# Return totals of two tiles made in one GpSimd addition, in a macaron block of two feed-forward layers around a quaternion memory

## The reference, cut to what matters

```python
keys = (x @ Wk.T + bk).reshape(B, L, 64, 4)
keys = keys / max(norm(keys, axis=-1), 1e-12)
values = (x @ Wv.T + bv).reshape(B, L, 64, 4)
bound = quat_mul(values, keys)
memory = jnp.cumsum(bound, axis=1)
retrieved = quat_mul(memory, quat_conj(keys)).reshape(B, L, D)
retrieved = retrieved / jnp.sqrt(positions)[None, :, None]
normed = layernorm(retrieved) * ln_g + ln_b
return x + (normed @ Wo.T + bo)
```

## Time and profile before

| What | Value |
|---|---|
| Time, median of 3 runs | 648.37 us (646.26 to 649.11) |
| Profiled execution: time | 648.11 us |
| Profiled execution: span of its instructions | 646.4 us |
| Mean granted TensorE clock | 0.994 |
| VectorE busy, whole span | 565.1 us (87%), 1168 instructions |
| GpSimd busy, whole span | 539.8 us (84%), 626 instructions |
| PE busy, whole span | 612.6 us (95%) |

### The profile page before, as it was taken

The page is one execution under the profiler, slowest core; times in us unless marked ns, Lnnn a source line. Parts: engine busy times, 40 slices in busy tenths (PEclk is TensorE's granted clock), DMA queues, the critical chain, the costliest instruction groups (busy, mean ns, idle before and its releaser), DMA issues.

```text
span 646.4 us, 12285 instructions
## 1 busy us (share of the span) xinstructions
PE 612.6 (95%) x3341; PEld 521.1 (81%) x3341; DVE 565.1 (87%) x1168; ACT 468.2 (72%) x858; POOL 539.8 (84%) x626
## 2 busy tenths in 40 slices
PE   6989999999987999999999999998877999999997
PEld 5878989989865787777878787777666899898996
DVE  6979999998869999999999999999848788787773
ACT  5666776767567888888888888887365777677662
POOL 4588898897848999999999999998826988889863
PEclk9989999999999999999999999999899999999999
DMA  8740000000000000000000000000000110110111
GB/s 251 238 132 1 0 0 0 0 0 1 1 1 1 1 2 0 0 0 0 0 0 0 0 0 0 0 1 0 2 0 2 67 65 32 65 65 32 65 66 66
DMA packets 19273, 18.66 MB, mean 29 GB/s; under 512 B 1328, under 2 KB 19248, under 8 KB 19248
## 3 DMA queue, kind: packets, MB, share of 16 engines
q1 hardware_dynamic: 19248, 18.36, 8.8%
HBM read 9.97 MB, written 8.39 MB: 28 GB/s over the span
## 4 chain that ended last, share of the span: by engine, by line
PE 45%; POOL 25%; issue 18%; DVE 7%; ACT 3%; POOLq 1%; DMA 0%; DVEq 0%; ACTq 0%
PE bank L1228 25%; PE bank L1259 16%; POOL rhalf L286 7%; POOL ret L293 6%; POOL kact L275 5%; POOL bhalf L268 4%; PE bank L1242 4%; POOL bhalf L266 1%; ACT xn L778 1%; POOL rhalf L284 1%; DVE xk L410 1%; POOL xr_lo L1084 1%; DVE xn L613 1%; DVE kact L418 0%; POOL rstd L1077 0%
## 5 line engine op out<-in xcount | busy, mean ns | idle before, releaser
L1259 PE MATMUL bank<-wffn,kact 128*128 128x256 f32 x512 | 118.0, 384 | 6.5 <-DVE kact L418 4.1
L1318 PE MATMUL bank<-wkv,m_xnT 128*128 128x256 f32 x480 | 116.4, 385 | 2.4 <-ACT m_xnT L882 2.4
L1259 PEld LDWEIGHTS bank<-wffn,kact 128*128 128x128 f32 x512 | 96.0, 192 | 19.5 <-DVE kact L418 4.5
L1318 PEld LDWEIGHTS bank<-wkv,m_xnT 128*128 128x128 f32 x480 | 88.8, 190 | 24.2 <-ACT m_xnT L882 8.8
L299 POOL TENSOR_TENSOR xk_lo<-xk,xk_hi 128x1024 fp32r<-128x1024 f32 x30 | 71.1, 2370 | 43.7 <-ACT xk_hi L786 43.4
L1091 POOL TENSOR_TENSOR res<-res,gating_buffers 128x1024 f32 (+1 forms) x31 | 74.6, 2408 | 13.5 <-DVE gating_buffers L425 13.0
L1084 POOL TENSOR_TENSOR xr_lo<-xr,xr_hi 128x1024 fp32r<-128x1024 f32 x32 | 76.0, 2374 | 7.6 <-ACT xr_hi L792 6.2
L613 DVE TENSOR_TENSOR xn<-bank,khat 128x1024 f32<-128x1024 f32 x64 | 77.7, 1216 | 2.2
L778 ACT ACTIVATE xn<-res,shift,rstd 128x256 f32 (+1 forms) x128 | 66.5, 592 | 15.3 <-POOL shift L1079 11.0
L613 DVE TENSOR_TENSOR gating_buffers<-bank,khat 128x1024 f32<-128x1024 f32 x64 | 77.4, 1211 | 0.0
L1228 PE MATMUL bank<-wffn_hi,xr_hi 128*128 128x256 f32 x256 | 72.1, 282 | 0.0
(11 more groups left out here) (135 smaller groups left out, 1603.8 us busy)
## 6 DMA issues: line engine op xcount, KB each, us to landing
res<-x SPq DMA_DIRECT2D x15, 512.0 KB, 4.2
out<-res SPq DMA_DIRECT2D x15, 512.0 KB, 2.9
res<-x SPq DMA_DIRECT2D x2, 256.0 KB, 2.9
out<-res SPq DMA_DIRECT2D x2, 256.0 KB, 2.2
wffn<-w_k SPq DMA_DIRECT2D x1, 256.0 KB, 4.6
wffn<-w_r SPq DMA_DIRECT2D x1, 256.0 KB, 5.3
wo<-w_o SPq DMA_DIRECT2D x1, 256.0 KB, 5.6
wffn<-w_v SPq DMA_DIRECT2D x1, 256.0 KB, 5.8
```

The source lines that it names most:

```text
L1259: last = nc.tensor.matmul(dst[:, i, :], x[:, f, i * P:(i + 1) * P], wffn[:, w, f, :], start=f == 0, stop=f == FC - 1)
L1318: last = nc.tensor.matmul(dst[:, i, :], m_xnT[:, f, i * P:(i + 1) * P], wkv[:, f, col:col + D], start=False, stop=f == FC - 1, skip_group_ ...
```

## The change

The totals of the return of both tiles of a step are made in one addition of 2 x 256 = 512 elements. It stands where the total of tile 1 stood, in the next step behind the first half of the bind sum of tile 0; the total of tile 0 at the end of its own step is left out. One semaphore counts the merged totals instead of one for each tile. VectorE's ln_stats waits for it once, ahead of the statistics of tile 0. ret_half waits for it before it writes rhalf again. retrieve waits for the second return half instead of the total, before it writes the products again.

```diff
-        rprod_done, rhalf_done, ret_done = for_tiles("rprod"), for_tiles("rhalf"), for_tiles("ret")
+        rprod_done, rhalf_done, ret_done = for_tiles("rprod"), for_tiles("rhalf"), sem("m_ret_done")
...
                 engine.wait_ge(rprod_done[i], s + 1)
-                need(engine, ret_done[i], s)
+                need(engine, ret_done, s)
...
-        def ret_total(engine, j, b, i):
+        def ret_total(engine, j, b):
+
             s = 2 * j + b
-            engine.wait_ge(rhalf_done[i], s + 1)
+            for i in range(2):
+                engine.wait_ge(rhalf_done[i], s + 1)
             need(engine, m["normed_done"], s - 1)
-            engine.tensor_tensor(ret[:, b, i, :], rhalf[:, i, 0, :], rhalf[:, i, 1, :], ALU.add).then_inc(ret_done[i], 1)
+            engine.tensor_tensor(ret[:, b, :, :], rhalf[:, :, 0, :], rhalf[:, :, 1, :], ALU.add).then_inc(ret_done, 1)
...
                     need(dve, m["normed_done"], s - 1)
+                    dve.wait_ge(ret_done, s + 1)
                     for i in range(2):
-                        dve.wait_ge(ret_done[i], s + 1)
                         nc.vector.bn_stats(n_st[:, b, i, :], ret[:, b, i, :]).then_inc(m["st_done"], 1)
...
                     s = 2 * j + b
-                    need(dve, ret_done[i], s)
+                    need(dve, rhalf_done[i], s)
                     dve.wait_ge(upto_done[i], s + 1)
...
                         if behind:
-                            ret_total(nc.gpsimd, *at(j, b, -1), 1)
+                            ret_total(nc.gpsimd, *at(j, b, -1))
                         if ahead:
                             bind_half(nc.gpsimd, *at(j, b, 1), 0, 1)
...
                         if ahead:
                             bind_half(nc.gpsimd, *at(j, b, 1), 1, 0)
-                        ret_total(nc.gpsimd, j, b, 0)
                         if ahead:
                             bind_half(nc.gpsimd, *at(j, b, 1), 1, 1)
...
-            ret_total(nc.gpsimd, NP - 1, 1, 1)
+            ret_total(nc.gpsimd, NP - 1, 1)
```

## The result

The changed kernel takes 673.66 us, the median of four runs (672.57 to 677.05), against 648.74 us for the kernel before in its four (646.26 to 649.18). The ratio is 1.040, with a 95% interval of 1.035 to 1.045. The forecast was 674.4 us, in a range of 669.5 to 680.5.

A forecast was written before the change was run, and what follows sets the result against it. VectorE was taken to set the step, in a loop with GpSimd's total; 29 x 0.88 + 0.47 = 26.0 us on top of 648.37 us gave 674.4 us, range 669.5 to 680.5.

The forecast's parts named there:

- The loop: VectorE's bind product, GpSimd's bind half and total, VectorE's statistics to next bind product form a loop giving the 8.54 us step.
- The price of 512 elements: GpSimd's merged total: 1.28 us, from a line between additions of 256 and 1024 elements.
- The bounds of 1.19 and 1.46: Limits in us for GpSimd's merged total: half a 1024 addition, and two additions of 256.
- The sum per step: VectorE's statistics 0.88 us late per step: 0.56 from the longer addition, 0.32 from the first statistic's lost cover.
- The sum: Whole memory stage: 29 steps at 0.88 us plus 0.47 for step 3, 26.0 us slower.
- The saving at step 3: At step 3 GpSimd's bind half was 0.41 us late; one addition fewer removes that, so it pays 0.47 us.
- GpSimd's relief is worth nothing: GpSimd's saving of 0.14 us per step falls into its gap before bhalf L266, only lengthening its idle time.
- the rival in which GpSimd bounds: Memory stage: 31 merged totals save 0.14 us each, 4.3 us in all, giving 644.1 us; chance 3%.
- The rival of no change: VectorE has 0.88 us of slack after the statistics, so the time stays 648.4 us, by 1; chance 2%.
- VectorE catches up in part: Small gaps on VectorE, 0.16 us a step, make good part of the stall: 669.6 us; chance 10%.
- More than the sum: PE's added idle time lowers its clock in stretches, or the total is dearer: 677 to 682 us; 8% above 680.
- the old wait: VectorE's wait for tile 1's total before the second statistic, already 0.1 to 0.16 us in every step.

The follow-up runs named there:

- e1: Changed kernel with VectorE taking the statistics behind bind(s+1, tile 1) instead of ahead of it: 647.01 us, ratio 1.000.
- e2: Changed kernel with GpSimd's merged total ahead of the first bind half instead of behind it: 647.46 us, ratio 1.001.
- e5: Changed kernel with the merged total one addition further back, behind both bind halves of tile 0: 694.32 us, ratio 1.069.
- e3: Kernel before with both totals in the next step, as two additions of 256, and retrieve waiting for the second return half: 670.48 us, ratio 1.037.
- e8: Kernel before (two totals of 256) with VectorE's statistics behind bind(s+1, tile 1): 648.45 us, ratio 0.999.
- e6: e2 with ScalarE copying the transposed input out ahead of the bias copy into the keys' bank: 645.94 us, ratio 0.995.
- e7: Kernel before with ScalarE copying the transposed input out ahead of the bias copy into the keys' bank: 648.19 us, ratio 1.000.
- e4: Kernel before with only retrieve's wait changed, to the second return half instead of the total: 648.03 us, ratio 1.001.

## Why the prediction was right, point by point

**The loop.** Shown. The wait was forecast before the statistics, as about 0.95 us in 30 steps, some 28 us in all; it is 0.94 to 1.02 and 29.4 us, in 30 waits. Taking it away at either end (e1, e2) gives all of the loss back, and one addition more inside the loop (e5) adds 0.68 us a step, 694.3 us where 693.7 was expected.

**The price of 512 elements.** 1.28 us was taken from a line between 256 and 1024; it is 1.272. The bounds of 1.19 and 1.46 were not needed. The estimate from the Trainium skill (GPSIMD Engine Reference, section 3.1) was 1.241 us, 0.03 too low. Its slope held: from 256 to 512 elements it is (1272 - 731)/256 = 2.11 ns an element, and 2.12 by the Trainium skill's figures.

**The sum per step.** 0.88 us was forecast and 0.91 measured. Most of the 0.03 between them is the wake of VectorE, the time from the end of GpSimd's addition to the start of the statistics: I took 0.04 us, and it is 0.10 in every second step (316.54 to 316.64) and 0.03 in the others (324.75 + 1.28 = 326.03 to 326.06).

**The sum.** 26.0 us were forecast for 30 steps, and the medians differ by 24.9. That this is so close is partly luck. The 26.0 us from the first khat to the last hold only 29 of the 30 pairs, for which the forecast has 28 x 0.88 + 0.47 = 25.1; with the measured terms all 30 come to 29 x 0.91 + 0.60 = 27.0, an estimate, so the sum was about 1 us too low. The stretches outside the steady steps, of which the first stage alone differs by some 3 us between profiled executions, hide that.

**The saving at step 3.** 0.41 was forecast and about 0.3 came: the interval there grew from 8.78 to 9.38 us, by 0.60 where the others grew by 0.87 to 0.94. The reason given, one addition fewer, isn't needed for it. In e3, with all twelve additions, the same interval grew by 0.36 instead of 0.69: the longer steps ahead of it already let GpSimd come up.

**GpSimd's relief is worth nothing.** Shown by e1 against e8: with the statistics out of the way, eleven and twelve additions give the same time. That excludes the rival in which GpSimd bounds and the 4.3 us that it promised. The rival of no change falls with the wait itself: VectorE had no slack behind the statistics.

**VectorE catches up in part.** Refuted: the gaps before and behind khat are the same with the stall as without it. This rival should have had less than 10%.

**More than the sum.** Not seen in the steady steps: the granted clock was 1.00 from 222 to 443 us. One stretch of the kind that this rival names did come, from 208 to 211 us, and the two intervals between khat that it touches grew by 1.24 and 0.87 us, at most 0.3 more than others. That it belongs to the change is not shown; the last section has what the runs say.

**Where I was incomplete.** I wrote that VectorE sets the step and that the loop through the total gives its 8.54 us. The loop is right, but if it alone set the step, the step would fall to 8.40 us once the wait is gone. It falls to 8.53 (e2), about the length of the loop through the keys. The sum didn't need this, since a loop that grows by 0.9 us leaves the other behind, but a forecast of e1 or e2 by the old wait alone would have promised 4 us that are not there. The gap of GpSimd was also put in one place (1.2 us before L266). It came in two, 0.74 there and 0.54 before L284 (0.81 and 0.38 in every other step), as tile 1's return product is late by the same stall. Last, the prediction has the chain in the two feed-forward stages on PE alone; the view of the chain shows that only from 37 us on in the first and from 500 us on in the third, and ahead of these it runs over VectorE, ScalarE and GpSimd too.

## What to carry to other kernels

Merging two small instructions saves a little time on the engine that runs them, here 0.15 us a step (2 x 0.69 against 1.23 us from start to start). It also makes the first half's result come no sooner than the second's, and the reader waits for the longer instruction before it can start on either. So follow the result's reader back to the input of the merged instruction. Where the reader's own engine makes something that the merged instruction must wait for, the two engines form a loop, and if that loop sets the step, all that the instruction grows by is paid in every step, whatever the busy shares are. A wait too short to stand in the list of waits, such as the 0.14 us seen only in the start-to-start times of a pair, can mark such a loop. When it is opened, expect the next loop before counting a gain.

## What the runs showed of the hardware that was not expected

The granted clock of PE fell in short stretches whose number and place differ between executions. In the profiled run of the kernel before, one such stretch lies in the first stage (37 to 42 us), which the profiled run of the changed kernel lacks. That one has another early in the memory stage, where PE had waited 2.19 us before 207.81. Windows of the two kernels, before and then after:

```profile
37.00:42.00 5.00, 4.56 (x13) 3.71 (x14) 4.82 (x19) 2.45 (x3) 4.89 (x3) 0.66 0.60 189
```

```profile
37.00:42.00 5.00, 5.00 (x29) 4.35 (x28) 4.78 (x20) 3.16 (x5) 4.92 (x5) 1.00 0.60 194
...
205.00:208.00 3.00, 0.81 (x5) 0.39 (x5) 3.00 (x9) 2.61 (x8) 3.00 (x6) 1.00 0.00 0
208.00:211.00 3.00, 2.86 (x12) 1.93 (x11) 2.93 (x5) 1.55 (x4) 1.34 (x2) 0.65 0.00 0
```

The stretch in the first stage accounts for a good part of its 3.0 us. The same 16 matmuls (L1259 before, L1260 after) took 5.41 us from 37.44 in the kernel before and 3.72 us from 36.15 in the changed one, so 1.7 us lie in them and 1.3 us in their later start, whose cause is open. The other profiled runs fit: the five that show 0.66 in this window (the kernel before, e2, e6, e7, e8) reach the first khat after 184.7 to 186.3 us, and the four with 1.00 up to 42 us (the changed kernel, e1, e4, e5) after 182.8 to 183.2, though the edits don't touch the first stage. e3 has its stretch earlier (0.81 from 10 to 15 us) and gets there after 185.5. How much of the spread of the kernel before, from 644.88 to 653.31 us, such stretches make was not measured.

The stretch behind 208 us may belong to the change. The profiled runs of e3 and e5, the other two kernels with a longer step, have one from 211 to 214 us (0.51 and 0.70), after PE had waited 2.00 and 2.87 us; the kernel before, e1, e2, e4, e6, e7 and e8 have 1.00 from 208 to 214 us. With one profiled run of each this is not shown. Inside the steady steps the clock stayed at 1.00, its upper level, while PE's busy time from 222 to 443 us fell from 217.57 to 197.92 of 221 us, and in e5 to 184.76.
